# Four graph layers over one 8192 x 8192 matrix: own features turned on VectorE in 32x32 squares instead of by ScalarE copies and TensorE transposes

## The reference

```python
h = relu(layernorm(x))
for k in range(2):                       # layer 0: sweeps 1 and 2
    h = tanh(concat([adj @ h, h], axis=1) @ W0[k])
x = x + h
h = relu(layernorm(x))                   # layer 1: sweep 3
x = x + adj @ (h @ W1) + bias
h = relu(layernorm(x))                   # layer 2: sweep 4
x = x + adj @ (h * (u >= 0.1) / 0.9)
h = relu(layernorm(x))                   # layer 3: sweep 5
deg = sum(adj, axis=1)
x = x + concat([h, (adj @ h) / (deg + 1)], axis=1) @ W3.T
```

## Time and profile before

| | |
|---|---|
| median of 3 runs | 2378.01 us (2377.7 to 2378.52) |
| the profiled execution | 2377.46 us |
| its span, first to last instruction | 2375.3 us |
| TensorE busy | 2323.9 us, 98% |
| VectorE busy | 1052.3 us, 44% |
| ScalarE busy | 139.1 us, 6% |
| read from HBM | 817.20 MB, 345 GB/s over the span |
| granted TensorE clock, mean | 0.999 |

### The profile page before, as it was taken

One profiled execution on the slowest core, in us unless ns is written; L12 is line 12 of the kernel. 1 busy time (PEld: TensorE's weight loads), 2 busy tenths in 40 slices (PEclk: granted clock), 3 DMA queues, 4 the chain that ended last, 5 costly groups with the idle time before them and its releaser, 6 DMA issues.

```text
span 2375.3 us, 23517 instructions
## 1 busy us (share of the span) xinstructions
PE 2323.9 (98%) x9540; PEld 1140.0 (48%) x9540; DVE 1052.3 (44%) x2111; ACT 139.1 (6%) x315; POOL 9.9 (0%) x22
## 2 busy tenths in 40 slices
PE   6899999999999999999999999999999999999998
PEld 3444445444445444444444444444454444444655
DVE  7865656555554211100089878877321100005311
ACT  1000000000001311100010000000000000000000
POOL 0000000000000000000000000000000000000000
PEclk9999999999999999999999999999999999999999
DMA  9999999999998788888869888886899999999998
GB/s 382 421 421 374 378 353 379 357 380 348 375 381 306 279 292 297 295 300 300 346 255 365 302 306 311 314 337 250 318 378 371 372 372 357 363 372 374 367 422 356
DMA packets 118491, 820.84 MB, mean 346 GB/s; under 512 B 14448, under 2 KB 18672, under 8 KB 19184
## 3 DMA queue, kind: packets, MB, share of 16 engines
q1 hardware_dynamic: 113904, 814.79, 89.3%
q10 hardware_dynamic: 3712, 2.46, 0.3%
q0 software_dynamic: 768, 2.10, 0.3%
HBM read 817.20 MB, written 2.10 MB: 345 GB/s over the span
## 4 chain that ended last, share of the span: by engine, by line
PE 92%; DMA 6%; DVE 2%; issue 0%; ACT 0%; SPq 0%; DVEq 0%
PE double_acc L604 57%; PE spare L604 12%; PE single_acc L580 12%; PE spare L580 8%; DMA ring<-in_adj 5%; PE natural L653 1%; DMA resid<-in_x 1%; PE natural L657 1%; PE spare L628 1%; DVE centred L780 0%; DVE deg_part L817 0%; DVE deg_part L816 0%; DVE stats L768 0%; DVE moments L771 0%; PE natural L651 0%
## 5 line engine op out<-in xcount | busy, mean ns | idle before, releaser
L604 PE MATMUL double_acc<-ring,operand 128*128 128x512 f32 x3144 | 1368.9, 593 | 3.1 <-DVE operand L929 1.6
L604 PEld LDWEIGHTS double_acc<-ring,operand 128*128 128x128 f32 x3144 | 589.9, 190 | 727.1 <-issue 718.8
L580 PE MATMUL single_acc<-ring,operand 128*64 128x256 f32 x3008 | 357.0, 386 | 39.3 <-DVE operand L794 22.5
L861 DVE TENSOR_TENSOR sums<-double_acc,sums 64x256 f32<-64x256 f32 x120 | 50.6, 421 | 703.0 <-PE double_acc L604 702.2
L604 PE MATMUL spare<-ring,operand 128*128 128x512 f32 x672 | 299.6, 599 | 0.0
L580 PEld LDWEIGHTS single_acc<-ring,operand 128*64 128x64 f32 x3008 | 206.0, 137 | 191.4 <-issue 37.0
L816 DVE TENSOR_TENSOR deg_part<-deg_part,ring 128x1024 f32<-128x1024 f32 x214 | 262.2, 1225 | 7.3 <-DMA ring<-in_adj 0.2
L817 DVE TENSOR_TENSOR deg_part<-deg_part,ring 128x1024 f32<-128x1024 f32 x214 | 262.1, 1225 | 7.4
L834 DVE TENSOR_TENSOR partial<-spare,partial 64x256 f32<-64x256 f32 (+1 forms) x190 | 80.4, 423 | 277.1 <-PE spare L604 135.5
L604 PEld LDWEIGHTS spare<-ring,operand 128*128 128x128 f32 x672 | 124.2, 190 | 156.8 <-issue 156.8
L580 PE MATMUL spare<-ring,operand 128*64 128x256 f32 x1456 | 163.5, 381 | 0.9 <-DVE partial L834 0.9
(11 more groups left out here) (59 smaller groups left out, 561.8 us busy)
## 6 DMA issues: line engine op xcount, KB each, us to landing
ring<-in_adj SPq DMA_DIRECT2D x756, 1024.0 KB, 6.5
held<-in_adj SPq DMA_DIRECT2D x17, 1024.0 KB, 8.9
resid<-in_x SPq DMA_DIRECT2D x16, 128.0 KB, 16.6
kept<-in_adj SPq DMA_DIRECT2D x2, 1024.0 KB, 10.9
for_layer<-in_u POOLq DMA_DIRECT2D x16, 128.0 KB, 2.4
out_rows<-for_layer ACTq DMA_DIRECT2D x16, 128.0 KB, 6.9
w_both_sb<-in_w_both ACTq DMA_DIRECT2D x2, 80.0 KB, 11.4
w_own_sb<-in_w_own ACTq DMA_DIRECT2D x2, 32.0 KB, 12.7
```

The lines of the kernel that those rows point to most:

```text
L580: last = nc.tensor.matmul(acc[half_of(h), 0:HALF], operand[:, b.j * TPB + t, half_of(b.row.half)], stream[:, t, nodes_of(h)], start=b.firs ...
L604: last = nc.tensor.matmul(acc[:, :], operand[:, b.j * TPB + t, :], stream[:, t, :], start=b.first and t == 0, stop=b.last and t == TPB - 1)
L861: last = nc.vector.tensor_tensor(to, got[own, nodes_of(h)], to, ALU.add)
```

## The change

The turn is done by VectorE alone. Each 32 x 32 square of the row's own features is transposed from `operand` straight into its place in `own_t`: 16 instructions a turn, each with two squares (32 partitions x 64 elements). `pair_own`, `own_by_pair`, the semaphores `turned` and `own_paired`, TensorE's transposes and ScalarE's second copy are gone, and the turn no longer uses a spare bank. VectorE's turn stands at the turn's place in `PLAN`, and it waits for the row's operand and, from r = 2 on, for the post of row r - 2, which reads the same half of `own_t`.

```diff
@@ kinds_with_banks
-        if kind in ("added", "turn") or what == "degree" and of is DEGREE_ROWS[-1]:
+        if kind == "added" or what == "degree" and of is DEGREE_ROWS[-1]:
@@ tensor engine
-            def turn(row):
-
-                wait_new(consts_loaded, 16 * CONSTS)
-                wait_new(own_paired, rows_with_own(row.r))
-                acc = next_spare()
-                for k in range(2):
-                    last = nc.tensor.transpose(acc[:, k * P:(k + 1) * P], own_by_pair[:, k, :], ident[:, :])
-                last.then_inc(turned, 1)
-
             def post(row):
...
+                wait_new(consts_loaded, 16 * CONSTS)
                 if row.own:
                     wait_new(own_ready, rows_with_own(row.r))
@@ scalar engine
-            def pair_own(row):
-
-                wait_operand(act.wait_ge, row.sweep, row.i)
-                own = operand[:, tiles(row.i), half_of(row.half)].rearrange("p (h k) f -> p k h f", k=2)
-                nc.scalar.copy(own_by_pair[:, :, :].rearrange("p k (h f) -> p k h f", h=2), own).then_inc(own_paired, 1)
...
-                elif what == "turn":
-                    if row.r == (SWEEPS - 1) * NB:
-                        pair_own(row)
-                    act.wait_ge(turned, rows_with_own(row.r))
-                    use = SPARE_USES.index(("turn", rows_with_own(row.r) - 1))
-                    nc.scalar.copy(own_t[:, slot, :], spare[use % 2][:, 0:HALF]).then_inc(own_ready, 1)
-                    if row.i != (0 if row.sweep == SWEEPS else NB - 1 if row.sweep == 1 else 0):
-                        pair_own(ROWS[row.r + 1])
@@ vector engine
+            def turn(row):
+
+                wait_operand(dve.wait_ge, row.sweep, row.i)
+                if row.r >= 2:
+                    dve.wait_ge(posted, row.r - 1)
+                own = operand[:, tiles(row.i), half_of(row.half)].rearrange("p (h k) f -> p h k f", k=2)
+                to = own_t[:, row.r % 2, :].rearrange("p (k n) -> p k n", k=2)
+                for h in range(2):
+                    for c in range(F // SQUARE):
+                        strip = slice(h * F + c * SQUARE, h * F + (c + 1) * SQUARE)
+                        for q in range(QUARTERS):
+                            part = slice(q * SQUARE, (q + 1) * SQUARE)
+                            last = nc.vector.transpose(to[strip, :, part], own[part, h, :, c * SQUARE:(c + 1) * SQUARE])
+                last.then_inc(own_ready, 1)
...
+                elif what == "turn":
+                    turn(of)
```

More of the change, by code:

```diff
@@ L424, in gnn_kernel @@
         own_t = sb("own_t", [P, 2, HALF])
-        own_by_pair = sb("own_by_pair", [P, 2, 2 * F])
         deg_part = sb("deg_part", [P, 2 * BLOCK])
@@ L458, in gnn_kernel @@
         blocks_used = sem("blocks_used")
-        turned = sem("turned")
         posted = sem("posted")
@@ L480, in gnn_kernel @@
         own_ready = sem("own_ready")
-        own_paired = sem("own_paired")
         tanh_ready = sem("tanh_ready")
@@ L597, in next_spare @@
                     what, count = SPARE_USES[n - 2]
-                    wait_new({"added": added_taken, "turn": own_ready, "degree": deg_taken}[what], count + 1)
+                    wait_new({"added": added_taken, "degree": deg_taken}[what], count + 1)
                 return spare[n % 2]
@@ L680, in _ @@
                     multiply[of.kind](of).then_inc(blocks_used, 1)
-                elif what in ("turn", "post"):
-                    {"turn": turn, "post": post}[what](of)
+                elif what == "post":
+                    post(of)
                 elif what == "degree" and of is DEGREE_ROWS[-1]:
@@ L712, in _ @@
                 act.dma_start(to[:], of[:]).then_inc(consts_loaded, 16)
-            pair_own(ROWS[0])
             for g in range(2, NGROUPS):
@@ L742, in _ @@
                         nc.scalar.activation(to, got, ACT.Tanh).then_inc(tanh_ready, 1)
-                        if row.r == NB - 1:
-                            pair_own(ROWS[NB])
                     if row.sweep in (2, 3, 4):
```

## The result

| | before | changed |
|---|---|---|
| median of six runs each, us | 2378.11 | 2387.03 |
| lowest to highest, us | 2377.7 to 2379.02 | 2382.47 to 2388.59 |
| profiled execution, us (span) | 2377.46 (2375.3) | 2388.46 (2386.7) |
| ratio, 95% interval | | 1.0035 [1.0024, 1.0045] |

The change costs 8.9 us in the medians, 0.38%. One thing has to be known to read the six times: they lie in two groups that go with TensorE's mean granted clock, 2382.5 and 2383.2 us at 0.999, and 2387.0 to 2388.6 us at 0.996 to 0.997. The profiled execution is of the second group.

The account below looks back on a forecast made before the run. TensorE's stream was taken to bound the kernel, except at the start and in sweep 5's load-bound second half. Terms 1.7 - 3.1 + 5.2 - 2.4 + 0.8 + 3.5 = +5.7, clock +2.6, together +8.3: 2386 us, range 2377 to 2392.

Parts of the forecast that it names:

- The turn, 4.1 us, no overlap: On VectorE, each turn's 16 transposes run one after another at 0.255 us each, 4.1 us a turn.
- Rival B: The VectorE transposes overlap as the statistics do, 2.1 us a turn, giving 2372.6 us; chance 0.10.
- Start, +1.7: First rows of sweep 1: turns 0 and 1 delay VectorE's sums, so row 1's post starts 1.7 us later.
- Rows 3 to 13, -3.1: Sweep 1: 11 transpose pairs leave TensorE at 0.28 us each, turns hidden in VectorE's 6.32 us wait; -3.1 us.
- Top of sweep 2, +5.2 without the clock: Short rows from row 16: uncovered turns delay sums and `finish`, and TensorE's blocks wait; +5.2 us.
- Rows 21 to 31, -2.4: Later sweep 2: four blocks or more hide turn and `finish`; eleven pairs removed at 0.22 us gain 2.4 us.
- Start of sweep 5, +0.8: A turn ahead of `finish` of sweep 4's last row delays a block by 1.1 us, less a pair: +0.8 us.
- Tail, +3.5: Kernel end: the turn after the last sums delays `finish` and the last four instructions by 3.5 us.
- Clock, +2.6 from two of three gaps: TensorE at half speed for 3.4 us after the two longest gaps (row 18's block, last post): +2.6 us.
- rival D: Whole kernel: the delays and gains without any clock drop, +5.7 us, 2383.7 us; chance 0.17.
- Covered or not: VectorE's turns cost only where a post or block needs it; a 6.32 us wait covers rows 3 to 13.

Follow-up runs that it names:

- e6: The change with each of the sixteen transposes reading and writing the same partition strip, both staying for four, data misplaced; 2376.49 us (one run).
- e12: The change with each transpose reading the strip behind the one it writes, both staying for four, data misplaced; 2375.84 us, ratio 0.9992.
- e7: The change with its sixteen transposes reordered: output strip changes with each, input strip stays for four, same result; 2383.21 us (one run).
- e3: The kernel before with only rows 64 to 79 (sweep 5) turned on VectorE; 2381.66 us, ratio 1.0018.
- e10: The change with sweep 2's turns, from its third row on, placed behind `finish` of the row before; 2381.57 us, ratio 1.0017.
- e11: The change with row 16's turn behind row 15's post, rows 18 on behind the previous row's finishing, last row's ahead of its block; 2375.80 us.
- e4: The kernel before with only rows 2 to 13 and 21 to 31 turned on VectorE; 2373.20 us, ratio 0.9982.
- e9: The kernel before with rows 2 to 15 and 17 to 31 turned on VectorE, from row 18 behind the previous row's finishing; 2371.85 us, ratio 0.9976.

## Why the prediction was right

The forecast of 2386.0 us, slower by over 0.2%, was met (2387.03), by the mechanism it named: turns of 4 us without overlap, paid where something waits for them. The sum of its terms came out less exactly than the total. By its steps:

- **The turn, 4.1 us, no overlap:** 3.98 us. The strips decided it, as I had argued from the earlier trace rows; each instruction was 0.25 us from the next instead of 0.255. Rival B's overlap exists (e6 and e12, 2.5 us, 0.13 us apart, the very pitch of its statistics) but not for these pairs of strips.
- **Start, +1.7:** +1.3 in the changed kernel, 0.9 to 1.6 in the five others with these turns. The post waited 1.70 us and started 1.2 us later. Loads stayed in time: from 60 to 130 us TensorE waited for them 6.5 us in all, before and after.
- **Rows 3 to 13, -3.1:** -1.9, in all eleven kernels that have these turns. Here the size was wrong, and the reason is known. I read the price of a pair as the distance to the post behind it, 0.28 us. But the pair also served as the post's run-up: behind a pair the post's first product leaves the second 0.22 us later (before, 260.21 to 260.43), behind a single block 0.33 us later (after, 261.03 to 261.36). Before and after:

```profile
260.21 0.39 PE L653 MATMUL natural<-w_both_sb,sums 128*128 128x128 f32 x2
260.43 0.39 PE L657 MATMUL natural<-w_own_sb,own_t 128*128 128x128 f32 x2
```

```profile
261.03 0.49 PE L642 MATMUL natural<-w_both_sb,sums 128*128 128x128 f32 x2
261.36 0.39 PE L646 MATMUL natural<-w_own_sb,own_t 128*128 128x128 f32 x2
```

  So 0.28 - 0.11 = 0.17 us a row. In sweep 2 the pair stood alone between double blocks, and there the 0.22 us were whole.
- **Top of sweep 2, +5.2 without the clock:** sized about 0.8 us too high. e7 has +5.1 with an estimated 0.9 us of clock in it, which leaves 4.2, or 4.4 without row 21's pair, which the forecast counts in the term behind this one. The profiled execution has +7.9 with 3.7 of clock. The first step was right: from block (14,15) on the account moves by 1.90 us until the post of row 16 (forecast 1.9). Behind it `finish` of row 17 came 4.5 and not 5.05 us later, since the two turns were 0.1 us shorter each and the small operations between them started 0.1 us closer than I had put them. The waits before the post of row 16, the block of row 18 and the last post were foreseen at 3.2, 3.9 and 4.0 us; they measured 3.01, 3.35 and 3.43.
- **Rows 21 to 31, -2.4:** -2.4. Their turns were covered, as were those of rows 3 to 13.
- **Start of sweep 5, +0.8:** the jump stands in all six kernels at 1.12 us (forecast 1.1, less a pair), and about 0.8 is what is left in the mean. The profiled execution has 2.6. Single executions differ by as much again in the stretch bound by loads.
- **Tail, +3.5:** 3.2 (e3, e7), or 4.0 with the half clock.
- **Clock, +2.6 from two of three gaps:** right in kind and too small for the profiled execution, where it took 4.5 us (3.7 and 0.8). The drop came behind all three gaps, and the one that I had left out, the shortest, was followed by the longest stretch of 1.2 GHz. It is a number that no execution has to keep: 3.6 us lie between two executions with the same turns. Four of the six had the lower mean clock (0.996 to 0.997), and that decided between my forecast and rival D (2383.7), near which the other two fell (2382.5, 2383.2). They are no proof of D's sum without a clock: e7, with their mean clock of 0.999, still has 0.9 us of it. The drop at 37 us in the trace before was worth nothing either way: the changed kernel doesn't have it and is 0.2 us ahead at the eleventh block.
- **Covered or not** was the heart of the matter, and the experiments show it from the other side: with the same instructions in other places e10 and e11 are 4.7 and 10.4 us under the change, and with turns in covered places alone e4 and e9 are faster than the kernel before.

How near the median came is partly chance. By stages the profiled execution adds 11.4 us to the one before, not 8.3: 1.2 from rows 3 to 13, 1.8 in sweep 5, 0.6 in the top of sweep 2, the tail and the clock together, less 0.4 at the start. The 0.6 hides two errors of opposite sign: by the table's stages the clock took 1.9 us more than I gave it, and the delays in the top of sweep 2 and the tail 1.3 less. The median of the six lies 1.4 us below that execution, and before's 0.65 above its profiled one.

## What to carry to other kernels

Work moved from a full engine to a half-idle one is paid where the half-idle one is waited for, not by its share: here 23 covered rows gave 4.35 us, and a handful of uncovered ones took 14 (1.3, 7.9, 0.8 and 4.0 at the four places, some 4.5 of it by the clock behind the waits). So ask of each instance what stands behind it in the new engine's order, give it the place behind whatever others wait for, and leave the few instances without such a place where they were. When an instruction is taken out of a pipelined stream, the distance to its neighbour isn't the gain, since the neighbour may inherit the start-up that it hid; and small operations that hop between partition strips should be priced at the unoverlapped pitch (here 0.25 us, not 0.13).

## What was unexpected in the hardware

- Of two executions with the same turns (in another order of the sixteen) and the same waits of 3.01 and 3.35 us, one ran at 1.2 GHz for 6.8 and 3.4 us behind them, the other for 3.4 us and not at all. I had reckoned with one length. The wait of 3.01 us was followed by half clock in all five kernels that have it. A wait of 1.44 us (e11) and one of 1.54 us (e6) at the same place were followed by none.
- VectorE's small transposes overlap, at 0.13 us from start to start, when both strips stay; a change of the output strip alone holds them as much as one of the input's (0.25 us). One transpose of 128x256 takes 0.44 us, a ninth of sixteen of 32x64 with the same elements.
